# Attention steps in pairs, sorted by the tiling mode of the matmuls, with heads divided by broadcast totals

## The reference, cut to what matters

```python
q = ln @ Wq                                  # 256 queries
kv = concat([xn @ Wkv, ln @ Wkv])            # 4096 + 256 = 4352 keys
sim = einsum('bhid,bhjd->bhij', rmsnorm(q) * d ** -0.5, rmsnorm(k))
sim = where(mask, sim, -max)
out = einsum('bhij,bhjd->bhid', softmax(sim), v)
x = x + out @ Wout + bout
```

## Time and profile before

| | |
|---|---|
| median of 3 runs | 781.3 us |
| the profiled execution's own time | 780.73 us |
| its span | 779.0 us |
| PE, DVE, ACT, POOL busy | 91%, 70%, 56%, 29% |
| attention, from the first `project` to the last `add_out` | 65.4 to 606.0 us |
| granted TensorE clock, mean | 0.945 of 2.4 GHz |

### The profile page before, as it was taken

How to read it: one execution, slowest core, us unless ns; L and a number is a source line. 1 busy time by engine, 2 the same in 40 slices (tenths; PEclk the granted TensorE clock), 3 DMA queues, 4 the chain that set the end, 5 groups by cost and what they waited for, 6 DMA issues and landing times. The chain is left out here.

```text
span 779.0 us, 15876 instructions
## 1 busy us (share of the span) xinstructions
PE 706.3 (91%) x5910; PEld 575.5 (74%) x5910; DVE 541.9 (70%) x1012; ACT 439.8 (56%) x985; POOL 226.8 (29%) x194
## 2 busy tenths in 40 slices
PE   1537999999999999999999999999998775799998
PEld 1436777777777777777777777777775664799997
DVE  5995777677767767777776776777776452666764
ACT  4445666666666666666665665666564321456552
POOL 3531332232223223223222322322221020164460
PEclk9958999999999999999999999999999655699999
DMA  6205300000000000000000000000000300455610
GB/s 192 80 30 142 99 1 3 1 21 2 1 22 1 2 1 21 2 1 22 2 2 21 2 2 1 9 1 2 2 1 1 109 1 4 159 163 174 203 54 15
DMA packets 27562, 30.61 MB, mean 39 GB/s; under 512 B 4313, under 2 KB 24930, under 8 KB 27490
## 3 DMA queue, kind: packets, MB, share of 16 engines
q1 hardware_dynamic: 24834, 28.26, 11.5%
q10 hardware_dynamic: 2656, 1.39, 0.6%
HBM read 29.38 MB, written 0.26 MB: 38 GB/s over the span
## 5 line engine op out<-in xcount | busy, mean ns | idle before, releaser
L837 POOL TENSOR_TENSOR k_rms<-k_ss,neg_half 128x4 f32<-128x4 f32 x136 | 136.9, 1007 | 379.7 <-DVE k_ss L784 379.7
L528 PEld LDWEIGHTS kv_ps<-w_pair,xn 128*128 128x128 f32 x1632 | 202.5, 190 | 52.8 <-issue 52.7
L528 PE MATMUL kv_ps<-w_pair,xn 128*128 128x256 f32 x1632 | 229.9, 290 | 5.1 <-PEq L179 5.1
L777 DVE SCALAR_TENSOR_TENSOR sum_ps<-probs,tile_mask,sum_ps 128x512 f32<-128x512 f32 x256 | 193.3, 755 | 19.0 <-ACT probs L725 1.7
L725 ACT ACTIVATE probs<-s_ps,minus_bound 128x512 f32<-128x512 f32 x272 | 172.2, 684 | 4.9 <-PE s_ps L636 2.3
L701 ACT ACTIVATE k_sq<-kv_ps 128x256 f32<-128x256 f32 x136 | 52.1, 383 | 191.4 <-PE kv_ps L528 191.4
L648 PE MATMUL o_ps<-probs,v 128*64 128x256 f32 x1088 | 147.5, 392 | 0.4 <-ACT probs L725 0.4
L636 PE MATMUL s_ps<-q_parts,kt 64*128 64x256 f32 x1632 | 131.2, 293 | 0.5 <-ACT probs L725 0.5
L636 PEld LDWEIGHTS s_ps<-q_parts,kt 64*128 64x128 f32 x1632 | 104.2, 184 | 23.6 <-issue 22.7
L648 PEld LDWEIGHTS o_ps<-probs,v 128*64 128x64 f32 x1088 | 66.1, 136 | 37.8 <-ACT probs L725 0.8
L788 DVE TENSOR_TENSOR kt<-kt_ps,kt 128x256 fp32r<-128x256 f32 x136 | 57.7, 424 | 49.3 <-ACT kt L717 49.2
(11 more groups left out here) (183 smaller groups left out, 676.5 us busy)
## 6 DMA issues: line engine op xcount, KB each, us to landing
w_raw<-in_ffn_W SPq DMA_DIRECT2D x18, 1024.0 KB, 5.3
p_rows<-in_ctx SPq DMA_DIRECT2D x8, 512.0 KB, 3.8
w_raw<-in_L_xattn_Wkv SPq DMA_DIRECT2D x14, 128.0 KB, 2.4
p_wq_raw<-in_L_xattn_Wq ACTq DMA_DIRECT2D x1, 1024.0 KB, 5.9
wout<-in_L_xattn_Wout SPq DMA_DIRECT2D x8, 128.0 KB, 2.1
x_res<-in_x SPq DMA_DIRECT2D x1, 256.0 KB, 4.4
w_raw<-in_L_xattn_Wkv ACTq DMA_DIRECT2D x2, 128.0 KB, 4.0
f_Wq<-in_L_attn_Wq SPq DMA_DIRECT2D x1, 256.0 KB, 3.7
```

What stands on the lines that cost most here:

```text
L528: last = nc.tensor.matmul(out, stationary(k, s), moving(k, m), start=n == 0, stop=n == len(terms) - 1)
L777: nc.vector.scalar_tensor_tensor(total[:], probs[n % 2][:, i], seen, sum_ps[:], ALU.mult, ALU.add).then_inc(sum_done, 1)
L837: nc.gpsimd.tensor_tensor(k_rms[n % 2][:].rearrange("p i c -> p (i c)"), k_ss[n % 2][:].rearrange("p i c -> p (i c)"), neg_half[:, 0:4], A ...
```

## The change

Each engine's loop now runs over pairs of steps m (steps a = 2m and a + 1). TensorE's order in a pair is: both transposes of the pair, the projections of the next pair, [the output product of an ended pass], the scores of the pair, `weight_v` of the pair before, [the totals of an ended pass]. `scores` alternates between two sets of two banks by the step's parity (four score banks). The transposed K has no bank of its own: both steps of a pair put it into the two banks of the even step, and wait for the exponentials that read them. The sum of weights lies in SBUF, in two buffers that alternate by pass, and is added to in place. `probs` has 4 buffers and `v` 6.

At a pass's end `totals` multiplies the sum of weights with a 128x64 block of ones, so that the totals of each head stand on all 64 of its partitions beside the heads' output. DVE inverts them as 128x256 (`normalise`), multiplies the heads' output with them on its way to SBUF, and one product with all 128 rows of Wout (`project_out`) gives both heads' share, which one instruction of DVE adds (`add_out`). ACT's copy `keep_out` is gone. For the pair in which pass g ended, `totals` comes 2 pairs later, `normalise` and `project_out` 3, `add_out` 4. The line numbers move: transposes are L633, scores L645, `weight_v` L657, `totals` L665, `project_out` L673, `scale_k` L756, additions L770 and L772, `mean_square` L778, `kt_rest` L782, the reciprocal L788, the product with it L792.

```diff
-    V_RING = 4
+    V_RING = 6
+    P_RING = 4
...
-        probs = ring(2, "probs", [P, 2, 2, NQ])
-        probs_sum = ring(1, "probs_sum", [P, 2, NQ])[0]
+        probs = ring(P_RING, "probs", [P, 2, 2, NQ])
+        probs_sum = ring(2, "probs_sum", [P, 2, NQ])
         heads_out = ring(1, "heads_out", [P, NQ])[0]
-        inverse = ring(1, "inverse", [P, 2, QT])[0]
+        inverse = ring(1, "inverse", [P, NQ])[0]
...
-        kt_ps = ctx.enter_context(nc.psum_tensor("kt_ps", [P, 512], F32))
-        s_ps = [ctx.enter_context(nc.psum_tensor(f"s_ps{c}", [P, 2, NQ], F32)) for c in range(2)]
-        o_ps = [ctx.enter_context(nc.psum_tensor(f"o_ps{b}", [P, 512], F32)) for b in range(2)]
-        sum_ps = ctx.enter_context(nc.psum_tensor("sum_ps", [P, 2, NQ], F32))
+        s_ps = [[ctx.enter_context(nc.psum_tensor(f"s_ps{h}{c}", [P, 2, NQ], F32)) for c in range(2)] for h in range(2)]
+        o_ps = [ctx.enter_context(nc.psum_tensor(f"o_ps{b}", [P, 2, NQ], F32)) for b in range(2)]
...
+        def kt_ps(n):
+            return s_ps[0][n % 2][:].rearrange("p i q -> p (i q)")[:, 0:2 * P]
+        def ended(m):
+            g = (2 * m + 2) // NU - 1
+            return g if 0 <= g < NPASS and ((g + 1) * NU - 1) // 2 == m else None
...
             def transpose_k(n):
                 pe.wait_ge(kn_done, n + 1)
-                if n:
-                    pe.wait_ge(kt_lo, n)
+                if n >= 2:
+                    pe.wait_ge(exp_done, 2 * (n - n % 2 - 2) + 1 + n % 2)
                 for i in range(2):
-                    last = nc.tensor.transpose(kt_ps[:, i * P:(i + 1) * P], kn[n % 2][:, i].rearrange("p c d -> p (c d)"), ident[:])
+                    last = nc.tensor.transpose(kt_ps(n)[:, i * P:(i + 1) * P], kn[n % 2][:, i].rearrange("p c d -> p (c d)"), ident[:])
                 last.then_inc(kt_done, 1)
             def scores(n):
                 g, b = n // NU, n % 2
-                pe.wait_ge(kt_lo, n + 1)
-                if n:
-                    pe.wait_ge(exp_done, 2 * n)
+                pe.wait_ge(kt_lo, n - n % 2 + 2)
+                if n >= 2:
+                    pe.wait_ge(exp_done, 2 * (n - 1))
                 for i in range(2):
                     for t, (s, m) in enumerate(((0, 0), (0, 1), (1, 0))):
                         for c in range(2):
                             half = slice(c * DH, (c + 1) * DH)
-                            last = nc.tensor.matmul(s_ps[c][:, i, :], kt[b][half, s, i * P:(i + 1) * P],
+                            last = nc.tensor.matmul(s_ps[b][c][:, i, :], kt[b][half, s, i * P:(i + 1) * P],
...
             def totals(g):
-                pe.wait_ge(out_kept, g + 1)
                 pe.wait_ge(sum_done, 2 * (g + 1) * NU)
                 for c in range(2):
-                    for j in range(QT):
-                        last = nc.tensor.matmul(o_ps[g % 2][:, c * QT + j:c * QT + j + 1], probs_sum[:, c, j * P:(j + 1) * P],
-                                                ones[:, 0:1], start=True, stop=True)
+                    last = nc.tensor.matmul(o_ps[g % 2][c * DH:(c + 1) * DH, 1, :], ones[:, 0:DH], probs_sum[g % 2][:, c, :],
+                                            start=True, stop=True)
                 last.then_inc(totals_done, 1)
-            def project_out(g, c):
-                if c == 0:
-                    pe.wait_ge(wout_in[g % 2], 16 * (g // 2 + 1))
-                    pe.wait_ge(inverse_done, g + 1)
-                else:
-                    pe.wait_ge(y_added, 2 * g + 1)
-                half = slice(c * DH, (c + 1) * DH)
+            def project_out(g):
+                pe.wait_ge(wout_in[g % 2], 16 * (g // 2 + 1))
+                pe.wait_ge(out_kept, g + 1)
                 for j in range(QT):
-                    last = nc.tensor.matmul(o_ps[g % 2][:, j * D:(j + 1) * D], heads_out[half, j * P:(j + 1) * P],
-                                            wout[g % 2][half, :], start=True, stop=True)
+                    last = nc.tensor.matmul(o_ps[g % 2][:, j, :], heads_out[:, j * P:(j + 1) * P], wout[g % 2][:], start=True, stop=True)
                 last.then_inc(y_done, 1)
...
+            for m in range(-1, STEPS // 2 + 1):
+                a = 2 * m
+                for n in (a, a + 1):
+                    if exists(n):
+                        transpose_k(n)
+                for n in (a + 2, a + 3):
+                    if exists(n):
+                        project(n)
+                if ended(m - 3) is not None:
+                    project_out(ended(m - 3))
+                for n in (a, a + 1):
+                    if exists(n):
+                        scores(n)
+                for n in (a - 2, a - 1):
+                    if exists(n):
+                        weight_v(n)
+                if ended(m - 2) is not None:
+                    totals(ended(m - 2))
             totals(NPASS - 1)
-            project_out(NPASS - 1, 0)
-            project_out(NPASS - 1, 1)
+            project_out(NPASS - 1)
...
             def weights(n):
-                if n >= 2:
-                    act.wait_ge(pv_done, n - 1)
-                    act.wait_ge(sum_done, 2 * (n - 1))
+                if n >= P_RING:
+                    act.wait_ge(pv_done, n - P_RING + 1)
+                    act.wait_ge(sum_done, 2 * (n - P_RING + 1))
                 for c in range(2):
                     act.wait_ge(s_done, 2 * n + 1 + c)
-                    nc.scalar.activation(probs[n % 2][:, :, c, :], s_ps[c][:], ACT.Exp, bias=minus_bound[:]).then_inc(exp_done, 1)
-            def keep_out(g):
...
+            for m in range(-1, STEPS // 2):
+                a = 2 * m
+                for n in (a, a + 1):
+                    if exists(n):
+                        keep_kt(n)
+                for n in (a + 2, a + 3):
+                    if exists(n):
+                        square(n)
+                        keep_v(n)
+                for n in (a, a + 1):
+                    if exists(n):
+                        weights(n)
+                for n in (a, a + 1):
+                    if 0 <= n // NU < NPASS - 1 and n % NU == 6:
+                        weights_hi(n // NU + 1)
...
-                        nc.vector.tensor_scalar(sum_ps[:], probs[n % 2][:, i], seen, None, ALU.mult).then_inc(sum_done, 1)
+                        if g >= 2:
+                            dve.wait_ge(totals_done, g - 1)
+                        nc.vector.tensor_scalar(total, probs[n % P_RING][:, i], seen, None, ALU.mult).then_inc(sum_done, 1)
                     else:
-                        total = probs_sum if u == NU - 1 and i == 1 else sum_ps
-                        if total is probs_sum and g:
-                            dve.wait_ge(totals_done, g)
-                        nc.vector.scalar_tensor_tensor(total[:], probs[n % 2][:, i], seen, sum_ps[:],
-                                                       ALU.mult, ALU.add).then_inc(sum_done, 1)
+                        nc.vector.scalar_tensor_tensor(total, probs[n % P_RING][:, i], seen, total, ALU.mult, ALU.add).then_inc(sum_done, 1)
...
-            def invert(g):
+                nc.vector.tensor_tensor(kt[n % 2][:, 1, :], kt_ps(n), kt[n % 2][:, 0, :].bitcast(F32), ALU.subtract).then_inc(kt_lo, 1)
+            def normalise(g):
                 dve.wait_ge(totals_done, g + 1)
                 if g:
-                    dve.wait_ge(y_added, 2 * g)
-                nc.vector.reciprocal(inverse[:].rearrange("p c j -> p (c j)"), o_ps[g % 2][:, 0:2 * QT]).then_inc(inverse_done, 1)
-            def add_out(g, c):
-                dve.wait_ge(y_done, 2 * g + c + 1)
+                    dve.wait_ge(out_kept, g)
+                nc.vector.reciprocal(inverse[:], o_ps[g % 2][:, 1, :]).then_inc(inverse_done, 1)
                 dve.wait_ge(inverse_done, g + 1)
-                if g or c:
-                    dve.wait_ge(y_added, 2 * g + c)
-                for j in range(QT):
-                    last = nc.vector.scalar_tensor_tensor(x_res[:, j, :], o_ps[g % 2][:, j * D:(j + 1) * D], inverse[:, c, j:j + 1],
-                                                          x_res[:, j, :], ALU.mult, ALU.add)
-                last.then_inc(y_added, 1)
...
+                if g:
+                    dve.wait_ge(y_done, g)
+                nc.vector.tensor_tensor(heads_out[:], o_ps[g % 2][:, 0, :], inverse[:], ALU.mult).then_inc(out_kept, 1)
+            def add_out(g):
+                dve.wait_ge(y_done, g + 1)
+                if g:
+                    dve.wait_ge(y_added, g)
+                nc.vector.tensor_tensor(x_res[:], x_res[:], o_ps[g % 2][:], ALU.add).then_inc(y_added, 1)
...
+            for m in range(-1, STEPS // 2 + 1):
+                a = 2 * m
+                for n in (a, a + 1):
+                    if exists(n):
+                        kt_rest(n)
+                if exists(a - 2):
+                    add_weights(a - 2)
+                for n in (a + 2, a + 3):
+                    if exists(n):
```

(77 more changed lines are left out.)

24 lines of the change are left out of this document (3 added, 21 removed).

## The result

The changed kernel takes 788.0 us (median of 4 runs, 787.37 to 789.26) against 780.91 for the kernel before on the same chip: the ratio is 1.009, with a 95% interval of 1.0072 to 1.0109. It is slower by 7 us. The forecast was 794, in a range of 781 to 806. The profiled execution has a span of 787.5 us, against 779.0.

A forecast was written before the change was run, and what follows sets the result against it. The prediction took TensorE, never waiting inside a pass, to bound the kernel. From the profiled 780.7 us, 780.7 - 36.7 - 11.4 + 42.7 + 18.2 = 793.5, or 794 us on the median's footing, range 781 to 806.

The forecast's parts named there:

- Pairs, -36.7 us: Two steps grouped on TensorE: three changes of tile shape instead of six, 6.94 us for 7.48, over 68 pairs.
- The 0.54 us of changes of shape: TensorE time lost per step at the three places where the matmuls' tile shape changes; 3.20 us of work remain.
- VectorE not the bound of a pair: K is scaled within 0.1 us of the transposes' need, so TensorE stays the bound; costed at nothing.
- A pass's end, -11.4 us: TensorE's totals and output product at a pass's end: 2.9 us falls to 1.3, for 7 passes inside the loop.
- The new wait, +42.7 us: TensorE's output product waits for VectorE's `out_kept`: 3.85 + 1.83 (reciprocal) + 0.42 (product) = 6.1 us, seven times.
- The clock, +18.2 us: After each of seven TensorE stalls, 5.2 us of work runs at half clock, costing 2.6 us each.
- Ends of the loop, 0: Last pass's tail, and draining and filling two steps at a time: 2 us less against 2 more, 3 either way.
- the clock fell in each of the seven waits: Rival denied here: TensorE's clock holds through the stalls, so the sum ends at 776 us; 8% chance.
- the reciprocal does not stream: Rival denied here: VectorE's reciprocal streams at 0.42 us, the stall is 4.7 us, total 784 us; 12% chance.
- VectorE is not the bound: Rival denied here: additions in SBUF take 0.80 us, VectorE bounds a pair, 13 us more, 807 us; 8% chance.
- the gain is the changes of shape: Its rival: the 0.54 us isn't changes of shape, a pair stays at 7.48 us, total 831 us; 2% chance.

## Why the prediction was right, step by step

- **Pairs, -36.7 us.** Measured per pair: 7.48 - 6.83 = 0.65, so 68 x 0.65 = -44. The 0.54 us of changes of shape are as forecast, and the run with two more of them a pair shows 0.34 for the two. The other 0.11 was not foreseen and is no change of shape: see the last section.
- **VectorE not the bound of a pair.** Right: no steady wait of the transposes for kn. Additions in place in SBUF took 748 ns against 750 assumed, but for seven of the 264, beside GpSimd's `weights_lo`, with 0.90 to 1.43 us; these lift the mean to 759. The sum of small parts that put the cover at about nothing was too careful by 0.25 to 0.4 us.
- **A pass's end, -11.4 us.** From the first product after a wait to the same one two passes on it is 135.90 us (224.06 to 359.96), where two passes took 133.0. 17 pairs give -11.1, two waits +11.1, and 4.74 and 5.66 us of work at half clock +5.2. The difference is +2.9, so the ends give 2.9 - 5.2 = -2.3, or -1.15 a pass where -1.6 was forecast, -8 in all. The run with the product one pair later shows what is missing. Its pairs with the totals are 0.43 us longer than their neighbours (7.18 for 6.75, 7.33 for 6.90), and its pairs with the product 0.89 (7.64 for 6.75), both as forecast (0.43 and 0.86). But in every second pass the product's pair takes 8.43, 0.8 more, with the late transposes: 0.4 a pass, which is the difference. The comparison of the passes points to the GpSimd instruction that the forecast mentions and costs at nothing, `weights_lo`, between the two roots and beside an addition; no run moved it. The changed kernel has the same in smaller form: of the 3.4 us of waits for kn in the list above, 2.3 are at the loop's start and 1.1 behind three of the passes' ends.
- **The new wait, +42.7 us.** Measured 7 x 5.53 = 38.7. The place, the cause and the count are right. These 5.53 us count from the modelled end of the last projection. Counted from starts, as the forecast does, the product starts 5.81 us behind the last projection, 5.7 later than it could: 7 x 5.7 = 40, which is also what separates the run with the clock kept up from the one without the wait. The reciprocal was put at 1.83 and takes 1.752 us. The chain ahead of it was 3.45 us from the last projection's start and not 3.85: 0.3 because the scaling of K of step a + 2 ended 1.75 us behind that start and not 2.05, and 0.1 by the overlap of VectorE's neighbouring instructions. Handing over from one instruction to the next, 0.2 us in all, was left out.
- **The clock, +18.2 us.** Measured: 38.4 us at half, 19.2 us; the run that keeps the clock up gives back 16.8.
- **Ends of the loop, 0.** From the first projection to that of step 6 it takes 22.1 us against 20.3, and from that of step 134 to the last addition 19.3 against 21.2: 1.9 us more and 1.9 less. The way in holds a loss of clock that the kernel before does not have: behind the first two waits of the transposes for kn (1.26 and 0.78 us, against one of 0.54 before) the clock fell again, and 3.41 us of work from 75.22 on ran at half, which costs 1.7.

The sum was 6 us too high: the pairs' gain was undersized by 7.5 and the wait oversized by 3 to 4. The other way go 3 at the passes' ends, 1 of the clock and 1 outside the attention (it begins at 66.9, not 65.4, in code that the change does not touch, and I did not follow that up). Of the rivals, none took place: the clock fell in each of the seven waits, the reciprocal does not stream, VectorE is not the bound, and the gain is the changes of shape. For the reciprocal, the line through two short rows was good to 5%. The Trainium skill's rule ("VectorE: DVE Perf Modes", "First, the fixed hardware budget"), read as eight cycles an element, would have made it 2.1 us; the trace does not bear that reading out, with 6.3 ns for each element from 4 to 256.

What the change does to this kernel is then two gains, 44 us from the pairs (37 from sorting by shape, 7 from the closer spacing of the matmuls, whose cause is open) and 6 to 8 from the new end of a pass, and one mistake in the order that takes 40 us in waiting and 17 to 19 in clock. Mended in either of two places, the kernel takes 730.7 us, 6.4% less than before.

## What to carry to other kernels

Sort a step's matmuls by tile shape: each change cost 0.14 to 0.20 us here, and grouping two steps halves their number. When an order is written out by hand on several engines, check for every wait where the giver has it in its own order, and not only that the data it starts from are old: the totals had been ready for a pair, but the division stood behind work that needs what TensorE had only just done. An engine that is otherwise mostly idle counts too: one GpSimd instruction between two roots went with transposes that were 0.2 to 0.6 us late here. A wait of 4 to 6 us on a TensorE that is otherwise never idle cost 1.5 times its length here (38.7 us of waiting, 19.2 of clock), because half the clock followed it.

## What was not expected of the hardware

In 26 of the 68 pairs of the changed kernel, mostly every second one between the waits, all 22 distances between the projections' matmuls behind the first distance are 0.113 to 0.114 us; in the others they are 0.117 to 0.119, which is also what nearly all steps of the kernel before have. The scores go with them: two steps of them take 1.56 us in a pair of the first kind and 1.61 in one of the second. A stretch keeps its spacing from one change of shape to the next; I saw none that changed it in between. It is why pairs take 6.75 or 6.90 us, and it is most of the 0.11 us a pair that the forecast missed. The run with scores and weights times V in turn has it in 11 of 68, the one with the product one pair later in 30. What sets it was not tried and stays open.

A second thing: where the sum of weights lies decides what an addition costs beside GpSimd. In SBUF, next to GpSimd's subtraction of 128x512, it took 1.23 to 1.24 us in the kernel before with the sum in SBUF alone, and 0.90 to 1.43 in the changed kernel; in PSUM, next to the same instruction, it stayed at 0.75.
